# The self-loop matrix of a relational graph layer: VectorE's one comparison becomes two ScalarE activations, made a group ahead

## What is computed

```python
h = jnp.maximum(_layernorm(x, axis=-1), 0.0)
out = h @ W_root + bias
for r in range(8):
    m = (edge_type == r)
    agg = segment_sum((h[src] @ W[r]) * m[:, None], dst, N)
    cnt = segment_sum(m, dst, N)
    out = out + agg / jnp.maximum(cnt, 1.0)[:, None]
return x + out
```

## Time and profile before

| | |
|---|---|
| median of 3 runs | 1065.55 us (1061.63, 1065.55, 1066.65) |
| profiled execution, its own time | 1065.97 us |
| its span from first to last instruction | 1064.2 us |
| granted TensorE clock, mean | 0.783 |
| busy: PE, DVE, ACT, POOL | 784.8, 800.8, 273.8, 774.6 us |
| chain that ended last | issue 37%, POOL 35%, DVE 10%, PE 7%, DMA 4%, ACT 1% |

### The profile page before, as it was taken

How to read it: one execution, slowest core, us unless ns; L and a number is a source line. 1 busy time by engine, 2 the same in 40 slices (tenths; PEclk the granted TensorE clock), 3 DMA queues, 4 the chain that set the end, 5 groups by cost and what they waited for, 6 DMA issues and landing times.

```text
span 1064.2 us, 19429 instructions
## 1 busy us (share of the span) xinstructions
PE 784.8 (74%) x4294; PEld 610.3 (57%) x4294; DVE 800.8 (75%) x2602; ACT 273.8 (26%) x672; POOL 774.6 (73%) x821
## 2 busy tenths in 40 slices
PE   0377777777778787877878778787777877778756
PEld 0256666556566565665656556565565655656545
DVE  8799999878887766867767676776767767767674
ACT  5632222222222222222222222222222222222200
POOL 7677777777777777777777777777777777777730
PEclk9988797887877877687787877878777787777865
DMA  8594222212222222222222222222222222222210
GB/s 261 159 228 95 55 55 58 54 54 57 55 57 56 56 57 54 56 54 54 56 54 57 54 55 56 54 56 54 56 55 53 56 55 57 55 54 56 54 34 6
DMA packets 51561, 70.85 MB, mean 67 GB/s; under 512 B 13843, under 2 KB 36662, under 8 KB 51526
## 3 DMA queue, kind: packets, MB, share of 16 engines
q0 software_dynamic: 25632, 52.55, 18.9%
q1 hardware_dynamic: 25894, 17.90, 6.4%
HBM read 63.99 MB, written 6.40 MB: 66 GB/s over the span
## 4 chain that ended last, share of the span: by engine, by line
issue 37%; POOL 35%; DVE 10%; PE 7%; DMA 4%; ACT 1%; SPq 1%; POOLq 0%; DVEq 0%; ACTq 0%
POOL hg L498 35%; PE acc L1458 4%; DMA hg<-h_table,idx 4%; PE fin L1491 2%; DVE onehot L1021 2%; DVE ring L1037 2%; DVE fin L1073 1%; DVE x_all L1121 1%; DVE blk L1079 1%; DVE loophot L1026 1%; PE acc L1462 1%; SPq L402 1%; DMA x_all<-in_x 1%; PE acc L1465 0%; PE zp L1480 0%
## 5 line engine op out<-in xcount | busy, mean ns | idle before, releaser
L498 POOL DMA_INDIRECT hg<-h_table,idx x741 | 712.1, 961 | 225.8 <-issue 219.7
L1458 PE MATMUL acc<-onehot,hg 128*128 128x104 f32 (+2 forms) x1602 | 486.9, 406 | 205.0 <-DMA hg<-h_table,idx 180.3
L1458 PEld LDWEIGHTS acc<-onehot,hg 128*128 128x128 f32 x1602 | 314.5, 244 | 323.5 <-issue 202.3
L1021 DVE TENSOR_SCALAR onehot<-iota,key_f 128x104 f32<-128x104 f32 (+2 forms) x801 | 234.1, 311 | 32.2 <-DVE ring L1037 17.0
L1462 PE MATMUL acc<-onehot,ones_bf 128*128 128x104 bf16 (+2 forms) x801 | 221.9, 277 | 0.0
L610 ACT ACTIVATE idx<-src_i 128x3 int32 (+1 forms) x247 | 50.7, 205 | 542.0 <-PE acc L1465 542.0
L1037 DVE TENSOR_TENSOR ring<-ring,acc 128x512 f32 x267 | 179.9, 674 | 2.7 <-PE acc L1465 2.6
L1491 PE MATMUL fin<-w_sb,blk 128*116 128x128 f32 x864 | 159.2, 332 | 0.0
L1121 DVE SCALAR_TENSOR_TENSOR x_all<-fin,inv,x_all 116x128 f32 (+1 forms) x400 | 137.0, 342 | 15.9 <-PE fin L1491 15.4
L1491 PEld LDWEIGHTS fin<-w_sb,blk 128*116 128x116 f32 x864 | 144.6, 236 | 1.1 <-issue 0.5
L1073 DVE SCALAR_TENSOR_TENSOR fin<-ring,zp 128x464 f32<-128x464 f32 x108 | 69.6, 645 | 83.9 <-PE zp L1473 77.5
(11 more groups left out here) (135 smaller groups left out, 390.5 us busy)
## 6 DMA issues: line engine op xcount, KB each, us to landing
hg<-h_table,idx POOLq DMA_INDIRECT x741, 2.5
out<-x_all SPq DMA_DIRECT2D x53, 58.0 KB
x_all<-in_x SPq DMA_DIRECT2D x7, 384.0 KB, 6.5
h_table<-h_all SPq DMA_DIRECT2D x7, 384.0 KB
h_all<-h_table SPq DMA_DIRECT2D x5, 504.0 KB
x_all<-in_x SPq DMA_DIRECT2D x5, 504.0 KB
hg<-h_table,src_i POOLq DMA_INDIRECT x36, 5.3
w_sb<-in_L_gnn_W SPq DMA_DIRECT2D x1, 512.0 KB
```

The lines of the kernel that those rows point to most:

```text
L498: nc.gpsimd.indirect_dma_start(out=hg[:, j, :], out_offset=None, in_=table, in_offset=bass.IndirectOffsetOnAxis(ap=idx[:, j:j + 1], axis=0 ...
L1021: nc.vector.tensor_scalar(onehot[:, t, 0:(e - a) * R].rearrange("p (r n) -> p r n", r=R), by_node[:, :, a:e], key_f[:, bass.ds(i * IT + t, ...
L1458: nc.tensor.matmul(both[:, 0, :, a:e], hg[:, slot, :], hot.rearrange("p (r n) -> p r n", r=R), start=(j == 0), stop=(j == n - 1), skip_gro ...
```

## The change

VectorE's comparison L1026 is taken out of `onehots`. ScalarE makes the matrix instead: |key − column| goes into a new buffer `loop_far` (f32, 96 x 256), and then relu(1 − that) into `loophot`, which is one where the key equals the column and zero elsewhere, as all are whole numbers. In step g of ScalarE's order the matrix of group g+1 is made, after `stage` and ahead of the step's other work; it waits for `group_summed` of the group that used the same of the five buffers. Both activations take their bias from a tensor; the second waits for the first through a semaphore.

```diff
@@ rgcn
+        loop_far = sb("loop_far", [GT * SLOTS, WIN])
@@ scalar
+            def loop_onehot(g, q, wait_for=None):
+
+                if wait_for is not None:
+                    act.wait_ge(loop_key_ready, wait_for)
+                if static(g):
+                    act.wait_ge(iota_made, 1)
+                    act.wait_ge(ones_made, 3)
+                elif not isinstance(g, int) or g >= GROUPS:
+                    act.wait_ge(group_summed, g - GROUPS + 1)
+                    settled(act)
+                if not static(g):
+                    act.wait_ge(loophot_ready, g)
+                    settled(act)
+                nc.scalar.activation(loop_far[:, :], iota[0:GT * SLOTS, :], ACT.Abs,
+                                     bias=loop_key[:, bass.ds(g, 1)], scale=-1.0).then_inc(loop_far_ready, 1)
+                act.wait_ge(loop_far_ready, g + 1)
+                settled(act)
+                nc.scalar.activation(loophot[:, q, :], loop_far[:, :], ACT.Relu,
+                                     bias=ones[0:GT * SLOTS, 0:1], scale=-1.0).then_inc(loophot_ready, 1)
@@ scalar, iteration
+                    if static(g):
+                        loop_onehot(g, q, 1)
+                    part_wait = PART_GROUPS.index(g + 1) + 1 if isinstance(g, int) and g + 1 in PART_GROUPS else None
+                    loop_onehot(g + 1, (q + 1) % GROUPS, part_wait)
@@ scalar, end
                 stage(EARLY - 1, GROUPS - 1, GROUPS)
+                loop_onehot(EARLY + 1, 1)
                 own(ENDB)
                 stage(EARLY, 0, GROUPS)
+                loop_onehot(EARLY + 2, 2)
                 take_counts(ENDB, slot_of(ENDB))
                 stage(EARLY + 1, 1, GROUPS)
+                loop_onehot(EARLY + 3, 3)
                 own_to_sbuf(ENDB)
+                loop_onehot(EARLY + 4, 4)
                 counts_to_sbuf(ENDB)
                 for b in LASTB:
+                    if b < LASTB[2]:
+                        loop_onehot(ENDG + b - LASTB[0], b - LASTB[0])
                     own(b)
@@ vector, onehots
-                nc.vector.tensor_scalar(loophot[:, q, :], iota[0:GT * SLOTS, :], loop_key[:, bass.ds(g, 1)], None,
-                                        ALU.is_equal).then_inc(loophot_ready, 1)
```

More of the change, by code:

```diff
@@ L258, in rgcn @@
         top_full, loops_T, loop_key_ready = sem("top_full"), sem("loops_T"), sem("loop_key_ready")
-        idx_ready, onehot_ready, loophot_ready = sem("idx_ready"), sem("onehot_ready"), sem("loophot_ready")
+        idx_ready, onehot_ready, loop_far_ready, loophot_ready = (
+            sem("idx_ready"), sem("onehot_ready"), sem("loop_far_ready"), sem("loophot_ready"))
         gathered = [sem(f"gathered{j}") for j in range(2 * IT)]
@@ L672, in iteration @@
                         act.wait_ge(zeros_made, 1)
[L673 to L677, removed]
+                    if not isinstance(g, int) or (AHEAD - 1) * GROUPS <= g - 1 < GALL - GROUPS:
+                        stage(g - 1, (q - 1) % GROUPS, GROUPS)
+                    elif (AHEAD - 3) * GROUPS <= g - 1 < (AHEAD - 2) * GROUPS:
+                        stage(g - 1, (q - 1) % GROUPS, 2 * GROUPS)
+                    if static(g):
+                        loop_onehot(g, q, 1)
+                    part_wait = PART_GROUPS.index(g + 1) + 1 if isinstance(g, int) and g + 1 in PART_GROUPS else None
+                    loop_onehot(g + 1, (q + 1) % GROUPS, part_wait)
                     if b is not None:
```

## The result

The changed kernel takes 1055.94 us (median of 6 runs, 1055.79 to 1057.75); the kernel before took 1064.51 us in 6 runs beside it (1061.63 to 1067.72). The profiled execution took 1057.02 us, with a span of 1055.1 and a mean granted TensorE clock of 0.785 (0.783 before).

The account below looks back on a forecast made before the run. GpSimd's unbroken gathers were taken as the bound. From the profiled 1065.97 us, 3.5 (gather lengthening), 0.3 (start) and 0.26 (tail) were subtracted, giving 1061.9 us, chance 0.45; range 1056.5 to 1067.

Parts of the forecast that it names:

- The bound: GpSimd's gathers run without a pause at a fixed pitch of about 1.25 us from 51 to 1024 us; TensorE follows.
- the pitch: GpSimd's gathers: 30 lengthened beside a `loophot` are freed of 0.116 us each, 3.5 us of 15.6 us lengthening.
- Rival 2: More is freed: one-hots and ring sums end before the next gather, half of 15.6 us goes; 1057.6 us, chance 0.25.
- The range: Forecast time 1056.5 to 1067 us, meant to take in the no-gain rival and most of the more-is-freed one.
- Rival 1: Collisions only dealt anew: a one-hot takes `loophot`'s place at a gather's start; 1065.4 us, chance 0.2.
- Rival 3: Slower: the shift puts one-hots on free gather starts in every iteration; one more each gives 1071.1 us, chance 0.07.
- Rival 4: ScalarE holds the kernel: 162 us more, 1228 us, or milder, a start 1 to 2 us later; chance 0.03.
- The port rule: VectorE and GpSimd block each other from shared ports for a whole instruction: 7.2 us saved instead of 3.5, 1058.2 us.
- VectorE's 94.5 us at nothing: 267 comparisons leave VectorE; in the steady part TensorE gains nothing, as the gather is late next.
- ScalarE at nothing: 267 activation pairs of 0.96 us, 256 us, added to ScalarE cost nothing, at most 1 us once.
- Start −0.3: The gather at 51.36 waits for TensorE's second group, which comes 0.26 us earlier: −0.3 us, +1 as other end.
- Tail −0.26: After the last gathers, one `loophot` at 1011.02 ahead of `make_block` leaves the path: −0.26 us.

Follow-up runs that it names:

- again_on_vector: The changed kernel with VectorE's old comparison put back in its old place, into a tensor nobody reads, while ScalarE still makes the matrix: 1064.84 us, ratio 0.9994.
- short_from_psum_2: The changed kernel with a short VectorE comparison from PSUM (96 x 64) ahead of each sum into the ring, on a usual chip: 1060.55 us, ratio 0.9971.
- same_from_psum: The changed kernel with one unread VectorE comparison of 96 x 256 per group, read from PSUM, ahead of the sum into the ring: 1060.40 us, ratio 0.9951.
- first_in_group: The changed kernel with the old comparison put back unread, ahead of the group's three one-hots instead of behind them: 1067.75 us, ratio 1.0023.
- the four runs: Doubled ScalarE work, short PSUM comparison, fold in four (changed kernel), bf16 comparison (kernel before), on another chip: 1337.04, 1345.17, 1344.96, 1322.87 us; kernel before there 1327.84.

## Why the prediction was wrong, point by point

- **The bound was right.** GpSimd's gathers, without a pause, set the time. Of the 9.1 us between the two spans, 8.2 are their lengthening, 0.5 the start and 0.4 what lies behind the last gather.
- **The step that failed is the pitch, "30 x 0.116 = 3.5 us"**, which measured 8.2. Its working took away the meetings of `loophot` itself and put those of all other operations at unchanged. For `loophot` alone it was about right: 28 gathers had lost 3.2 us beside it, and these are gone. What it left out is that VectorE's later operations move. At 300 to 990 us, of the gathers over 960 ns and counted above 944, the kernel before has 32 beside a one-hot, 3.2 us in all, and the changed one 10 and 0.4; beside `loophot` there were 19 and 2.2. Over the whole run one-hots give 3.4 of the 8.2 us, `loophot` 3.2, the folds of the ring's end 1.0 and the rest 0.6. The one-hots' share went with the removal and came back with the comparison (27 and 3.2 us in again_on_vector).
- **Rival 2 had the mechanism** (one-hots end before the next gather starts) and 1057.6 us, that is 8.4 us less than its profiled execution; measured were 8.2 in the gathers and 8.6 between the medians. It gave it 0.25 and the forecast 0.45. Its size was luck: "half of the 15.6" was not worked out from meetings. What spoke for its mechanism was in the text: the long gathers recur at one place of every second iteration, so a shift acts on all of them at once, and the 0.26 us of shift could have been held against the 0.17 us by which the one-hot at 609.92 reached into the gather.
- **The part below 300 us** gave 2.5 us of the 8.2. There the lengthening scatters from 4.6 to 9.7 us over the runs without an order that follows the edit (short_from_psum_2 has the most), so this share may be luck of place.
- **The range** ended at 1056.5, 1.1 us below rival 2, and was laid from one profiled execution that was 0.4 us above the median of three runs. The median of the six was 1 us lower again: rival 2's 8.4 us from there give 1056.1, below the range already.
- **Rival 1** (one-hots take `loophot`'s place) did not happen here. It happened in part in same_from_psum. **Rival 3** (a fixed collision that costs more) did not happen in the change; first_in_group shows the like of it, with 49 gathers lengthened beside one-hots in the steady part and 0.2% over the kernel before. **Rival 4** (ScalarE holds the kernel) did not happen.
- **The port rule.** The prediction held the row (0.12) against the whole overlap (0.24) and read it as half of a stop. The Trainium skill, "SBUF — State Buffer", "Who interferes with whom", says that the loser blocks fully until the other's instruction is done. The lengthened gathers above agree with that, if the gather asks for the ports 0.12 us after its recorded start. The 30 gathers that were not lengthened fit this badly: `loophot` had begun up to 0.055 us ahead of them and went on for 0.32 us. When exactly a gather takes the ports stays open. The estimate of 7.2 us by the rule was too high because it counted from the start. That ScalarE's work stops no gather is borne out by again_on_vector: the gathers are back at 962 ns, not above the 961 of before. And the engines do not meet only at semaphores, as is said at the start: here GpSimd and VectorE also met where neither waited for a semaphore.
- **VectorE's 94.5 us at nothing**: right as a load (TensorE's waits for one-hots fell only by 9 us, and those for gathers by 2 instead of growing; VectorE's busy time fell to 738.6 us and not to some 700). **ScalarE at nothing**: right; an activation is 507 ns, not 480, and the second starts 0.63 us behind the first. The least lead of the indices grew, from 1.8 to 4.1 us, since TensorE had summed the group earlier.
- **Start −0.3**: the wait at 51.36 fell from 0.99 to 0.70, as worked out; the one before it, which had not been reckoned with, from 0.73 to 0.53. **Tail −0.26**: 0.4 behind the last gather; no run takes this apart. The last wait of TensorE for a gather, which the prediction used as a mark at 1007.68 us with a tail of 56 us, ends at 1005.66 in the changed kernel, 49 us before the end, though what lies behind the last gather is only 0.4 us shorter: it is no stable mark.

## What to carry to other kernels

When one engine works through a queue at a fixed pitch, look at the spread of its own operations: the mean less the minimum, times the count, is the most that others take from it. Here it was 15.6 us, in an engine that never waited, and some 3 of them are no one's (the median lies 4 ns above the minimum). Here an operation of VectorE cost its own meetings and those of the operations that it delayed; the second share was the larger in the steady part (2.8 against 2.2 us), and it depends on place, so price the shift against the overlap of the meetings that recur. A shorter operation gave half of what moving it away gave (0.9958 against 0.9922), and one of the same size that read from PSUM cost 0.3% where the one from SBUF cost 0.7% (0.9951 and 0.9994 against 0.9922).

## What the runs showed of the hardware

- A gather that begins 0.09 to 0.10 us behind the start of a 96 x 256 comparison of VectorE from SBUF is lengthened by the overlap less 0.12 us (28 of 28 in the kernel before, 0.24 us of overlap); two other meetings, with 0.29 and 0.62 us of overlap, cost 0.17 and 0.50. One that begins up to 0.055 us behind it isn't lengthened (30 of 30), and the comparison takes up to 0.377 instead of 0.34 us. A comparison that begins some 0.6 us after a gather is longer as well (0.46 at 608.02).
- Beside a comparison of the same size from PSUM no gather was lengthened (116 began during one, 954 ns at most).
- A sum of two SBUF inputs stops a gather too (0.62 us of overlap, 0.50 more at 992.47).
- A comparison of 96 x 256 from PSUM takes 402 ns, from SBUF in f32 353, from bf16 292, and two ScalarE activations of that size 507 and 508.
- The shortest gather takes 940 ns on the usual chips and 943 in one run there; on the chip of the four runs it is 942 in three programs and 938 in one.
- On one chip the same kernel took 1328 us instead of 1065, and the order of the variants turned around.
